# Splitting the query weights one tile earlier, and rounding the last chunk of down weights three steps later

## The reference

```
n   = layernorm(x)
q   = rope(rms_norm(n @ wq))                  # 16 heads of 128
k,v = [ctx @ wk_ctx, rope(n @ wk)], [ctx @ wv_ctx, n @ wv]    # 4 groups of 128
x   = x + tanh(g0) * softmax(q k^T / sqrt(128) + mask) v @ wo
n2  = layernorm(x)
x   = x + tanh(g1) * ((silu(n2 @ gate_w * s1) * (n2 @ up_w * s2)) @ down_w * s3)
```

## Time and profile before

| | |
|---|---|
| median of 3 runs | 325.38 us (325.27 to 327.22) |
| profiled execution, its own time | 325.29 us |
| its span, first to last instruction | 323.4 us |
| TensorE busy | 297.3 us (92%) |
| ScalarE, VectorE, GpSimd busy | 231.9, 227.0, 182.6 us |
| mean granted TensorE clock | 0.989 |

### The profile page before, as it was taken

The page is one execution under the profiler, slowest core; times in us unless marked ns, Lnnn a source line. Parts: engine busy times, 40 slices in busy tenths (PEclk is TensorE's granted clock), DMA queues, the critical chain, the costliest instruction groups (busy, mean ns, idle before and its releaser), DMA issues.

```text
span 323.4 us, 6512 instructions
## 1 busy us (share of the span) xinstructions
PE 297.3 (92%) x2212; PEld 233.8 (72%) x2212; DVE 227.0 (70%) x477; ACT 231.9 (72%) x892; POOL 182.6 (56%) x178
## 2 busy tenths in 40 slices
PE   3777998996999999999999999999999999998866
PEld 1333566663777778888887888788878888777764
DVE  1357899889676688759987777658774765576454
ACT  2266687864687889897898768887887778776522
POOL 1154587566964467556874586456755685465320
PEclk9999899998999999999999999999999999999999
DMA  6999000000000010000100010000000000000001
GB/s 194 392 390 352 3 16 2 0 1 0 19 0 3 1 32 3 2 0 2 34 2 0 2 33 2 2 1 10 9 3 0 2 17 3 0 2 16 2 1 34
DMA packets 6721, 12.84 MB, mean 40 GB/s; under 512 B 801, under 2 KB 4257, under 8 KB 6689
## 3 DMA queue, kind: packets, MB, share of 16 engines
q1 hardware_dynamic: 6400, 12.00, 10.3%
q10 hardware_dynamic: 288, 0.43, 0.6%
HBM read 11.38 MB, written 1.05 MB: 38 GB/s over the span
## 4 chain that ended last, share of the span: by engine, by line
PE 57%; DVE 16%; ACT 13%; issue 6%; POOL 4%; DMA 3%; ACTq 0%; DVEq 0%; POOLq 0%
PE ps_kv L392 7%; PE ps_scores L615 6%; PE ps_attn L655 5%; PE ps_y L434 5%; PE ps_y L439 5%; PE ps_transposed L412 5%; PE ps_q L392 4%; ACT probs L851 4%; PE ps_probs L412 4%; PE ps_ff L482 4%; PE ps_q L400 3%; ACT squares L684 3%; PE ps_ff L502 3%; DMA const<-in_constants_dram 2%; PE ps_kv L400 2%
## 5 line engine op out<-in xcount | busy, mean ns | idle before, releaser
L851 ACT ACTIVATE probs<-ps_scores,exp_bias,q_scale 128x128 f32<-128x128 f32 x128 | 56.8, 456 | 15.8 <-DVE exp_bias L1125 15.8
L1253 POOL TENSOR_TENSOR q_rot<-q_rot,q_sin 128x512 f32<-128x512 f32 x32 | 41.5, 1298 | 22.2 <-DVE q_sin L977 22.0
L1298 POOL TENSOR_TENSOR probs<-probs,row_inv 128x512 f32<-128x512 f32 x32 | 36.8, 1149 | 20.0 <-DVE row_inv L1185 19.9
L1204 POOL TENSOR_TENSOR q_scale<-ssq_eps,minus_half 128x4 f32<-128x4 f32 x32 | 38.4, 1199 | 10.3 <-DVE ssq_eps L1156 10.2
L1215 POOL TENSOR_TENSOR fuse_lo<-fuse,fuse_hi 128x256 fp32r<-128x256 f32 x21 | 15.4, 732 | 45.0 <-ACT fuse_hi L693 45.0
L684 ACT ACTIVATE squares<-ps_q 128x128 bf16<-128x128 f32 x128 | 33.9, 289 | 9.2 <-PE ps_q L392 3.3
L827 ACT ACTIVATE pt<-ps_probs 128x512 f32<-128x512 f32 x32 | 19.1, 598 | 22.6 <-PE ps_probs L412 22.6
L615 PE MATMUL ps_scores<-kt,qt 128*64 128x128 f32 x512 | 34.4, 279 | 0.0
L655 PE MATMUL ps_attn<-pt,values 128*128 128x256 f32 x128 | 33.4, 383 | 0.0
L615 PEld LDWEIGHTS ps_scores<-kt,qt 128*64 128x64 f32 x512 | 30.1, 141 | 0.0
L973 DVE TENSOR_TENSOR q_rot<-ps_q,rope 128x512 f32<-128x512 f32 x32 | 21.9, 686 | 11.2 <-ACT squares L684 11.2
(11 more groups left out here) (148 smaller groups left out, 873.5 us busy)
## 6 DMA issues: line engine op xcount, KB each, us to landing
q_raw<-in_wq_dram SPq DMA_DIRECT2D x4, 512.0 KB, 9.1
o_raw<-in_wo_dram SPq DMA_DIRECT2D x4, 512.0 KB, 10.6
ctx_t<-in_ctx_dram SPq DMA_DIRECT2D x8, 128.0 KB, 2.6
out_dram<-x_sb SPq DMA_DIRECT2D x8, 128.0 KB, 1.7
stage<-in_gate_w_dram SPq DMA_DIRECT2D x2, 384.0 KB, 10.7
stage<-in_up_w_dram SPq DMA_DIRECT2D x2, 384.0 KB, 11.7
x_sb<-in_x_dram SPq DMA_DIRECT2D x1, 768.0 KB, 13.6
stage<-in_down_w_dram SPq DMA_DIRECT2D x2, 384.0 KB, 11.6
```

What stands on the lines that cost most here:

```text
L851: last = nc.scalar.activation(probs[:, i, :], ps_s[:, i * P:(i + 1) * P], ACT.Exp, bias=exp_bias[:, i:i + 1], scale=q_scale[:, k % 2, i:i ...
L1204: return nc.gpsimd.tensor_tensor(dst, src, minus_half[:, 0:src.shape[1]], ALU.pow)
L1253: nc.gpsimd.tensor_tensor(q_rot[:, :, :], q_rot[:, :, :], q_sin[:, :, :], ALU.add)\
L1298: nc.gpsimd.tensor_tensor(probs[:, :, :], probs[:, :, :], row_inv[:, :].unsqueeze(2).broadcast_to([P, 4, P]), ALU.mult).then_inc(probs_rea ...
```

## The change

The query weights are used natively for two tiles instead of three, so the queries of tile 2 (steps 8 to 11, projected in steps 7 to 10) go from native to split, and the tokens of tile 2 are split in step 4. The splits move to other steps. The last chunk of down weights is rounded in step 8 instead of 5, so GpSimd writes the second half of `w_down` in step 9 instead of 6. The NaN matmuls go from step 5 to 4, and `down_row_scale` from the start of step 6 to step 5, behind `row_inv`.

| step | 5 | 6 | 7 | 8 | 9 | 10 | 11 | 12 | 13 | 14 | 15 | 16 |
|---|---|---|---|---|---|---|---|---|---|---|---|---|
| split before | | kv0 | kv1 | kv2 | kv3 q0 | q1 | q2 | q3 | o0 | o1 | o2 | o3 |
| split now | q0 | q1 kv0 | q2 kv1 | | q3 kv2 | kv3 | o0 | o1 | o2 | o3 | | |
| down chunk rounded before | 5 | | | | | | | | | | | |
| down chunk rounded now | | | | 5 | | | | | | | | |

```
-NATIVE_TILES = {"kv": (3, 3, 3, 3), "q": (3, 3, 3, 3), "o": (3, 3, 3, 3)}
-SPLIT_AT = {6: [("kv", 0)], 7: [("kv", 1)], 8: [("kv", 2)], 9: [("kv", 3), ("q", 0)], 10: [("q", 1)], 11: [("q", 2)],
...
+NATIVE_TILES = {"kv": (3, 3, 3, 3), "q": (2, 2, 2, 2), "o": (3, 3, 3, 3)}
+SPLIT_AT = {5: [("q", 0)], 6: [("q", 1), ("kv", 0)], 7: [("q", 2), ("kv", 1)], 9: [("q", 3), ("kv", 2)], 10: [("kv", 3)],
...
-ROUND_AT = {n: n for n in range(len(FF_CHUNKS))}
-NAN_AT = 5
+ROUND_AT = {0: 0, 1: 1, 2: 2, 3: 3, 4: 4, 8: 5}
+NAN_AT = 4
...
                 if at_step(u, k) not in SHORT_OF_VECTOR:
                     attention_low(u, k)
-                if at_step(u, k) == NAN_AT + 1:
-                    down_row_scale()
...
                     nc.vector.reciprocal(row_inv[:, :], row_sum[:, :]).then_inc(inv_ready, 1)
+
+                if at_step(u, k) == NAN_AT + 1:
+                    down_row_scale()
```

More of the change, by code:

```diff
@@ L44 @@
 WIDE = 4
-NATIVE_TILES = {"kv": (3, 3, 3, 3), "q": (3, 3, 3, 3), "o": (3, 3, 3, 3)}
-SPLIT_AT = {6: [("kv", 0)], 7: [("kv", 1)], 8: [("kv", 2)], 9: [("kv", 3), ("q", 0)], 10: [("q", 1)], 11: [("q", 2)],
-            12: [("q", 3)], 13: [("o", 0)], 14: [("o", 1)], 15: [("o", 2)], 16: [("o", 3)]}
+NATIVE_TILES = {"kv": (3, 3, 3, 3), "q": (2, 2, 2, 2), "o": (3, 3, 3, 3)}
+SPLIT_AT = {5: [("q", 0)], 6: [("q", 1), ("kv", 0)], 7: [("q", 2), ("kv", 1)], 9: [("q", 3), ("kv", 2)], 10: [("kv", 3)],
+            11: [("o", 0)], 12: [("o", 1)], 13: [("o", 2)], 14: [("o", 3)]}
 SPLIT_ORDER = [c for at in sorted(SPLIT_AT) for c in SPLIT_AT[at]]
-ROUND_AT = {n: n for n in range(len(FF_CHUNKS))}
-NAN_AT = 5
+ROUND_AT = {0: 0, 1: 1, 2: 2, 3: 3, 4: 4, 8: 5}
+NAN_AT = 4
 TOKENS_SPLIT_FROM = min(NATIVE_TILES["kv"][1::2] + NATIVE_TILES["q"])
```

## The result

| | before | changed |
|---|---|---|
| median, in the comparison after the prediction | 326.20 us (8 runs) | 322.53 us (8 runs, 322.10 to 324.19) |
| ratio | | 0.9894, 95% interval 0.9864 to 0.9924 |
| profiled execution | 325.29 us, span 323.4 | 322.41 us, span 320.6 |

The forecast was 321.9 us with a range of 319.9 to 324.3. The change makes the kernel about 1.1% faster, almost on the line between "faster by 1%" and "no change" on which the forecast lay. Executions of both kernels scatter over 2 us, in two groups: before, four lie at 325.27 to 325.53 and four at 326.88 to 327.34; after, six lie at 322.10 to 322.61 and two at 324.06 and 324.19. The means of the lower groups differ by 3.0 us (0.9%), the medians by 3.67, since more of the executions before fell in the upper group. So the terms are read from the traces, at marks inside them, and not from differences of medians.

What follows compares the result with a forecast made beforehand. The prediction took TensorE as the bound, on the chain from step 6 to step 15. Its terms, 2.49 + 1.54 + 1.28 - 1.95 = 3.36 us, came off 325.29 us, giving 321.9 us, range 319.9 to 324.3.

Steps and rivals of the forecast that it cites:

- wait for `xn`: Step 6: TensorE's wait for the feed-forward input of tile 0 shrinks from 3.06 to 0.57 us, a gain of 2.49.
- wait for `w_down`: Step 9: TensorE newly waits before the down projection, as GpSimd writes `w_down` behind the query addition; costs 1.95 us.
- clock and restart behind it: Step 6, behind TensorE's wait: the granted clock no longer falls, a gain of 1.54 us, bounds 0 and 1.72.
- four query projections: Steps 7 to 10: split projections take 1.40 us where native take 1.72, a gain of 1.28 us.
- steps 6, 7 and 10 to 16: Second splits in steps 6 and 7 are covered; later moved splits change nothing, step 16's wait included: 0 us.
- a `q_scale` held behind the split: Step 5: GpSimd's `q_scale` slowed by VectorE's split, delaying `xn` by 0.92 us; 322.9 us, chance 0.13.
- the lateness of 0.3 us: Steps 8 and 9: VectorE some 0.3 us later against TensorE, counted in the 1.95 us wait for `w_down`.
- Rival 1: Step 9: the new wait for `w_down` lowers the clock, costing another 1.54 us; 323.5 us, chance 0.15.
- Rival 4: Step 6: TensorE waits for `xn` as before since something else feeds it late; 326.0 us, chance 0.05.
- Rival 5: Steps 6 and 7: doubled splits exposed in full, 4.84 us, with clock falls of 3.08; 329.9 us, chance 0.08.
- Rival 3: Step 9: GpSimd's order leaves `w_down` ready in time, so 1.95 us come back; 320.0 us, chance 0.08.

Runs made afterwards that it cites:

- experiment 4: Kernel before with only the tokens of tile 2 split as well in step 4, which nothing reads: 327.05 us, ratio 1.0006.
- Experiment 5: Changed kernel with GpSimd's second half of `w_down` ahead of the query addition in step 9 and `x_inv` ahead of `q_scale` in step 5: 319.97 us.
- experiment 3: Changed kernel with chunk 5 rounded in step 5 again, query weights still split a tile earlier: 326.88 us, ratio 1.0032 to the kernel before.
- experiment 6: Changed kernel with the split of q3 moved from step 9 to step 7, three splits there: 324.46 us, ratio 0.9947 to the kernel before.
- experiment 1: Changed kernel with GpSimd writing the second half of `w_down` ahead of the query addition in step 9: 320.71 us, ratio 0.9836 to the kernel before.

## Why the prediction came out right, point by point

The mechanism came as forecast: a shorter wait for `xn` with no fall of the clock, four cheaper projections, and a new wait for `w_down`. The size was less good than the number looks. In the two traces the same operation of step 16 stands at 171.62 before and 168.77 after: 2.85 us less, where the sum said 3.36. That the medians show the forecast 1.1% is in part luck, since they compare more executions of the upper group before than after. Term by term (the measured terms add up to 2.90):

| step of the prediction | forecast | measured | from |
|---|---|---|---|
| wait for `xn` | -2.49 | -2.15 | 3.06 to 0.91 |
| clock and restart behind it | -1.54 | -1.40 | start of `xn`'s turn to start of `ps_y`: 3.50 before, 2.10 after |
| four query projections | -1.28 | -1.28 | 1.40 for 1.72 |
| wait for `w_down` | +1.95 | +1.93 | 1.67, and 0.26 of restart |
| steps 6, 7 and 10 to 16 | 0 | 0 | TensorE without a wait up to step 16, and 0.75 for 0.74 there |

**The wait for `xn`** was mis-sized by 0.34 us, from errors that partly cancel. VectorE would have been ready at 75.6, over 0.4 us before the forecast's start of `xn`: the token split, taken as 0.42, cost nothing (experiment 4), and `q_lo` took 1.23 us, not 1.37, while VectorE's part of step 5 ran 0.2 us later than before (`x_var` at 73.95, 73.75 before). That 0.2 comes with the NaN matmuls, which the prediction put at 0: every kernel here that has them in step 4 starts the attention product of that step 12.50 us behind the mark, the two that have them in step 5 at 12.31. But `x_inv` was ready only at 75.68 and, above all, `xn` took 0.71 us longer beside GpSimd's product. The prediction had GpSimd as a rival here with another mechanism, a `q_scale` held behind the split. That did not happen: `q_scale` began at 73.91, ahead of the split at 74.03, and took 1.01 us, as the earlier trace rows had it for that order of starts. Experiment 5 shows the mechanism that I missed and that it was worth 0.7 us at this wait.
The Trainium skill (GPSIMD Engine Reference, Specifications) says that GpSimd shares its SBUF interfaces with VectorE and contends with VectorE instructions that read two SBUF inputs or run in a 2-port perf mode. The measured 1.11 us of `xn`, an instruction with one SBUF tensor, against 0.40 agrees with it, if `xn` runs in such a mode, which no run here shows.

**The clock** did not fall behind the shorter wait, as forecast. 1.54 counted the whole stretch; 1.40 is what the same operations took less, with the restart after 0.91 us in it.

**The query projections** gave what the rows said, to the hundredth. But experiment 3 shows what the sum hid: the term holds only with the place in VectorE's step 5 free.

**The wait for `w_down`** came at its place, behind the named operation on the named queue. The size is right by luck in its parts: the wait itself was 0.28 shorter than said, and a restart of 0.26 was not in the sum. The 0.28 is the lateness of 0.3 us that the sum gave VectorE: it did not come, the query addition ended 6.93 us behind the last attention product (109.18 - 102.25), 6.92 before (113.31 - 106.39).

**Rival 1**, the clock behind the new wait, did not come in the profiled execution. It did in experiment 6, behind 2.14 us. The row that it leaned on does not hold by itself: the changed kernel has the same wait of 1.94 us in step 2, until 30.04, and its clock stays at 1.00 there. **Rival 4** did not come, since the wait fell to 0.91. **Rival 5** did not come: ScalarE was busy for 9.04 of 9.22 us in step 7 and held nobody up, and even a third split of 1.05 us there exposed only 0.47 (experiment 6). **Rival 3** did not come by itself, but experiment 1 made it, with the 0.28 us for `q_lo` that stood behind. The prediction had said of q3, split in step 9 and read in step 10, that it was as before for the other chunks; in the changed kernel it is covered only because the wait for `w_down` comes first.

## What to carry to other kernels

When a piece of work is moved off the chain, look up its reader and the queue of the engine that writes for it: here 4.4 us of VectorE's work left the place ahead of `xn`, which was worth 2.15 us of wait and 1.40 of clock, and 1.9 came back since the last 1.8 us of the same work stood behind another operation on GpSimd, in the step that reads it. Two orders on GpSimd, with no work removed, gave 2.5 us more (experiments 1 and 5). When a wait goes, look for the next one that it covered. And test halves of a change apart: a part that gives 1.3 us in a sum may lose when it stands alone.

## What the runs showed of the hardware that was not expected

- The wait of TensorE for `w_down` cost more than itself: the matmul group behind 1.67 us of idle time shows 1.69 us instead of 1.43, at full clock. The ends of matmuls are modelled, but the starts agree: without the wait, the attention product behind it starts 1.93 us earlier (experiment 1), that is 1.67 + 0.26.
- Behind a wait of 3.06 us TensorE ran at half clock for some 3.1 us, behind 4.42 and 5.19 us for 5.31 and 5.34 us; behind 2.14 us in one trace for 3.4, starting 0.7 us after the restart, and behind 1.66 and 1.67 us not at all. Behind a wait of 1.94 us near the start the clock fell in the trace before and did not in the changed kernel's.
- `xn`, 128x256, took 0.40 us or 1.11 us by whether GpSimd's 128x512 product had begun 0.08 us before it; `w_down` 1.81 or 2.41 us, `x_inv` 0.79 or 1.50. Work that another engine stretches is slack that a timeline without gaps does not show (`exp_bias`, 0.73 or 0.41, with its end 0.03 us behind that of GpSimd's addition both times).
